# Attention's six middle batches: a hardware loop, or written out one behind the other

## The reference

```python
mod = (silu(c) @ wmod).reshape(8, 6, 1, 256)        # sa, ca, ga, sb, cb, gb
h = layernorm(x) * (1 + ca) + sa
q, k, v = split(h @ W_qkv + b_qkv)                  # 16 heads of 16
scores = q @ k.T / sqrt(16) + rel_bias[clip(i - j + 256, 0, 512)]
x = x + ga * ((softmax(scores) @ v) @ W_out + b_out)
h = layernorm(x) * (1 + cb) + sb
top2 = normalised top 2 of softmax(h @ gate_w.T + expert_bias)
out = layernorm(sum over the two experts of weight * (gelu(h @ w_up) @ w_down)) + h
x = x + gb * out
```

## Time and profile before

| | |
|---|---|
| median of 3 runs | 1375.01 us (1366.27 to 1378.25) |
| the profiled execution | 1366.95 us, its span 1365.3 us |
| mean granted clock of TensorE | 0.911 of full speed |
| busy: PE / PEld / DVE / ACT / POOL | 1129.6 / 896.5 / 803.5 / 640.6 / 864.6 us |
| first score of batch 0; of batch 1; last score of batch 7 | 83.2; 160.9; 779.5 us |

### The profile page before, as it was taken

The page is one execution under the profiler, slowest core; times in us unless marked ns, Lnnn a source line. Parts: engine busy times, 40 slices in busy tenths (PEclk is TensorE's granted clock), DMA queues, the critical chain, the costliest instruction groups (busy, mean ns, idle before and its releaser), DMA issues. The chain is left out here.

```text
span 1365.3 us, 33167 instructions
## 1 busy us (share of the span) xinstructions
PE 1129.6 (83%) x11290; PEld 896.5 (66%) x11291; DVE 803.5 (59%) x2057; ACT 640.6 (47%) x910; POOL 864.6 (63%) x955
## 2 busy tenths in 40 slices
PE   5559999898897998989989851499999999999910
PEld 3236776676676766766767630288888888888810
DVE  4535668467476684675766728555555555555557
ACT  4237776575675765766767611122222222222212
POOL 3235587477575874776756643757666776766656
PEclk9679999899998998999999955599999999999965
DMA  9497674753566447535553217024243344342364
GB/s 310 177 167 228 215 176 123 155 120 97 137 130 118 139 121 154 131 99 137 132 96 137 69 58 277 24 41 108 46 108 82 72 108 101 53 108 46 46 156 130
DMA packets 123113, 168.28 MB, mean 123 GB/s; under 512 B 13016, under 2 KB 99288, under 8 KB 123008
## 3 DMA queue, kind: packets, MB, share of 16 engines
q1 hardware_dynamic: 103136, 137.59, 37.6%
q0 software_dynamic: 19872, 29.15, 11.4%
HBM read 105.74 MB, written 60.96 MB: 122 GB/s over the span
## 5 line engine op out<-in xcount | busy, mean ns | idle before, releaser
L821 DVE CUSTOM_DVE_ANT_0 b_sn<-b_ps_s,s_tile 128x512 f32<-128x512 f32 x512 | 341.5, 688 | 233.7 <-PE b_ps_s L953 230.3
L752 ACT ACTIVATE b_pt<-b_ps_t 128x1024 f32<-128x1024 f32 x256 | 259.1, 1016 | 104.4 <-PE b_ps_t L967 102.6
L967 PE MATMUL b_ps_t<-b_ident,b_sn 128*128 128x128 f32 x2048 | 280.3, 281 | 4.8 <-POOL b_sn L643 3.2
L967 PEld LDWEIGHTS b_ps_t<-b_ident,b_sn 128*128 128x128 f32 x2048 | 248.5, 146 | 45.6 <-issue 16.7
L643 POOL TENSOR_SCALAR b_sn<-b_sn,b_mn 128x512 f32<-128x512 f32 x256 | 175.8, 699 | 145.4 <-DVE b_mn L821 144.7
L1557 ACT ACTIVATE d_g<-d_ps_u 128x512 f32<-128x512 f32 x156 | 92.8, 598 | 319.2 <-PE d_ps_u L1670 309.3
L744 ACT ACTIVATE b_sn<-b_sn,b_mn 128x512 f32<-128x512 f32 x256 | 182.3, 721 | 115.2 <-DVE b_mn L821 108.0
L953 PE MATMUL b_ps_s<-b_ks,b_qs 96*128 96x512 bf16 x512 | 184.8, 397 | 47.6 <-DVE b_mn L821 20.5
L1670 PE MATMUL d_ps_u<-d_xp,k_wu 128*128 128x256 bf16 x1776 | 202.3, 274 | 0.0
L1685 PE MATMUL d_ps_y<-k_wd,d_gp 128*128 128x256 bf16 x1776 | 199.9, 273 | 0.0
L1670 PEld LDWEIGHTS d_ps_u<-d_xp,k_wu 128*128 128x128 bf16 x1776 | 173.9, 99 | 21.8
(11 more groups left out here) (192 smaller groups left out, 1224.2 us busy)
## 6 DMA issues: line engine op xcount, KB each, us to landing
w_parts<-b_w_split SPq DMA_DIRECT2D x32, 512.0 KB, 3.4
splits<-b_parts SPq DMA_DIRECT2D x32, 384.0 KB, 2.6
b_qs<-splits SPq DMA_DIRECT2D x96, 128.0 KB, 6.0
b_ks<-splits SPq DMA_DIRECT2D x96, 128.0 KB, 7.8
b_w_raw<-in_w_up_t SPq DMA_DIRECT2D x16, 512.0 KB, 10.5
b_w_raw<-in_w_down_t SPq DMA_DIRECT2D x16, 512.0 KB, 6.9
k_wu<-w_parts SPq DMA_DIRECT2D x8, 1024.0 KB
k_wd<-w_parts SPq DMA_DIRECT2D x8, 1024.0 KB
```

Source lines behind the costliest of these rows:

```text
L752: act.activation(pt[:, m, 2 * pair:2 * pair + 2, :], ps_t[:, 2 * pair:2 * pair + 2, :], ACT.Exp).then_inc(exped, 1)
L821: dve.tensor_tensor_reduce(sn[:, n % 2, t, :], ps_s[:, t % 2, :], ahead.tile[:, n, at:at + S], -1.0, BIG, ALU.add, ALU.min, mn[:, n % 2, t ...
L967: mm = pe.transpose(ps_t[:, j, t * P:(t + 1) * P], sn[:, m, t, j * P:(j + 1) * P], ident[:, :])
```

## The change

`by_batches` loses its loop: a Python `range` over the eight batches calls `batch` with the same kinds in the same order, so that b is a constant everywhere, and each engine's program holds the middle batch six times. The loop's branch and its register work fall away; the instructions of a batch, their order, their waits' meaning and all tiles stay.

```diff
-        def by_batches(engine, batch):
-
-            batch(0, "first")
-            with engine.Fori(1, B - 1) as b:
-                batch(b, "middle")
-            batch(B - 1, "last")
+        def by_batches(batch):
+
+            for b in range(B):
+                batch(b, "first" if b == 0 else "last" if b == B - 1 else "middle")
...
-            by_batches(sp, batch)
+            by_batches(batch)
...
-            by_batches(pool, batch)
+            by_batches(batch)
...
-            by_batches(act, batch)
+            by_batches(batch)
...
-            by_batches(dve, batch)
+            by_batches(batch)
...
-            by_batches(pe, batch)
+            by_batches(batch)
```

## The result

| | before | changed |
|---|---|---|
| median | 1371.26 us (4 runs, 1366.27 to 1378.25) | 1333.15 us (4 runs, 1329.02 to 1334.35) |
| the profiled execution, its span | 1366.95, 1365.3 us | 1332.73, 1330.9 us |

The ratio is 0.9713 (95% interval 0.9659 to 0.9768): 38.1 us less by the medians, 34.2 us between the two profiled executions. With the further runs of the kernel before that the experiments brought, its median is near 1370 and the gain near 37.

A forecast was written before the change was run, and what follows sets the result against it. TensorE was taken to set each batch's pace, its branch stalls at five seams paid in full. Gain 30.8 us, other terms 0: 1336.2 from the profiled execution, 1344.2 from the median; forecast between them 1341, range 1329 to 1356.

The forecast's parts named there:

- The seam: Last job's start to head 1's first score, between batches: without TensorE's branch 5.65 us each, gaining 30.79 us over five.
- Rival A: At the seams, waits for h1 or the like give back part: 7.4 us, gain 20.2, time 1355; chance 0.14.
- The slow patch: Lower TensorE clock behind head 14's wait: three of six batches kept, cost 0; bounds 4.8 us gained, 3.2 lost.
- Instruction fetch: Written-out engines other than TensorE fetch some 7 packets in each of five more batches; cost taken as 0.
- rival C: Straight code starves DVE, ACT and POOL of instructions: 16.9 us lost a batch, some 1459 us; chance 0.04.
- Register work: Loop register instructions in the engines' sequencers go; no wait for them seen apart from the branch, gain taken as 0.
- Rival B: At the seams only branch time goes, nothing on the path; time stays at 1375; chance 0.04.
- Rival D: The slow patches in the batches vanish too: 4.8 us more gained, 1336 us; chance 0.08 for it or most.
- second stop: TensorE stopping again by "issue" 6.5 us after a seam's first score, for 0.94 us; part of the seam's cost.

The follow-up runs named there:

- e1: Changed kernel, but TensorE alone keeps the hardware loop, the other four engines written out: 1364.81 us, ratio 0.9963 to the kernel before.
- e2: Kernel before, but TensorE alone has its batches written out, the other four keep the loop: 1330.91 us, ratio 0.9708.
- e4: Kernel before, loop on all engines, the product with the values made for one key tile of four: 1318.33 us, one run.
- e9: The kernel before, unchanged, profiled a second time: 1368.09 us.
- e10: The changed kernel, unchanged, profiled a second time: 1330.10 us.
- e7: Changed kernel with the load of h1 moved from head 0 to head 0.5 on GpSimd: 1388.29 us, one run.
- e6: Changed kernel with one of VectorE's four normalising instructions moved from head 13 to 13.5: 1316.0 us, ratio 0.9624 to the kernel before.
- e5: Kernel before, loop on all engines, the product with the values made for three key tiles of four: 1360.31 us, one run.
- e8: TensorE alone in the loop, others written out, and SyncE issues the second stack's twelve loads two heads later: 1406.67 us, one run.

## Why the prediction was right

**The seam.** The step was right in place, cause and end value: 5.65 us was read from the seam without a branch and 5.58 came, six times. e1 and e2 show that TensorE's branch is the cause and the other engines' are not; e4 shows why. The sum over five seams, 30.8 us, came as 30.4 in the stretch that holds them. That close a match is partly luck of the pairing, since both figures take the kernel before from the same profile; between e9 and e10 the same stretch shrank by 37.3 us (463.90 to 426.62).

**The term that was too small.** The gain was 37 to 38 us by medians, where the forecast of 1341 against 1375 makes 34 and the sum 30.8. The price of a branch was taken from one profile that lay low: its five seams sum to 59.04, those of e9 and e1 to 63.96 and 63.8, and with 5.58 us as the end value the excess is 36.1 and 35.9 us, to which the longer heads behind the second gap add 1.2 (e9) and 2.6 (e1). I went halfway between the profiled execution and the median of the runs, 8 us apart, as if either kernel spread like that; part of it is likely a property of the branch, which the change removes. The time came out at 1333.15, 8 us below the forecast and 4 above the range's low end. The narrower reading also fits the narrower spread of the changed kernel (5 us against 12), but e9's other stretches show that the seams are not all of the spread.

**Rival A, h1.** Right to give it a price, and right that it would not come: no seam waited. The slack was read as 3 us; in the changed kernel h1 lands 3.1 to 5.0 us before q0 starts (issue and landing of L554 against the start of L996, batches 2 to 6). e7, which uses the slack up by moving the load 7.1 us, cost 55 us over six batches; the 7.4 us of the prediction could have held only for a load that is late by little.

**The slow patch.** Put at three of six, bounded by none and all. Four of batches 2 to 6 had one in the changed kernel's profile, three in its second. The cost of 0 was right within 1.6 us. Which batches have one remained open: e6 took away the wait and the patches, e7 the patches alone.

**Instruction fetch.** That q8 is TensorE's queue and q14 serves the others is shown by e1 and e2 together: over the whole span q8 has 82 packets and q14 has 40 where the others alone are written out, 68 and 23 where TensorE alone is. No wait of PE came from the new fetches, so rival C fell as reasoned. One sign of it can mislead: in the changed kernel the profile puts seven waits of POOL before b_v, 46.9 us, down to "issue". The kernel before has the same seven, 60.1 us, six of them put down to PE's b_ps_o; e2, whose POOL keeps its loop, has them at the length of the changed kernel (6.6 us a batch), and PE waits for none of them. The count was wrong: 17 packets more on q14, not 35. Of the seven packets of the first pass I took all as the body of one batch; the written-out batches need three to four each.

**Register work.** Put at 0; e2 shows 0.5 us a seam, through DVE at head 0, and seams of 5.58 in place of 5.65 where all is written out. Small and of the right sign.

**Rival B** fell with the result: the whole of the seams' cost came off the time, and no engine needed the idle time that went. Rival D, more patches gone, did not happen here, but came with e6.

**Two readings to correct.** The second stop in the earlier trace rows ends 6.5 us behind the first score; it begins at 5.6. And the prediction has DVE's 56 ns fit the 108 ns that the Trainium skill ("Advanced Engine Details and Errata", Control Flow Timing) gives for a compare-and-branch: 56 is half of it, and TensorE's branch, where its target needed no fetch (e4), took 215, twice as long. The measurements decide, each for its engine.

The landmarks: the last job (L1035, L1033 in the changed kernel) of batches 1 to 6 at 246.2, 332.0, 417.5, 501.9, 587.8 and 673.8 us, forecast from 245.5 to 672.8; the last score at 748.8, forecast 749.

## What to carry to other kernels

In this kernel a hardware loop was dear on the engine with by far the longest body (some 1970 recorded instructions a pass) and nearly free on the others (333 at most). So read the branch's row per engine, and the instruction queues in a window inside the loop. Where a queue went on fetching in every pass, each backward branch stalled its engine while the target came, amid the DMA traffic of the kernel's own loads; the cures seen here are to write the body out, or to make it shorter. And take a recurring price from more than one execution: here the first profile showed 59 us of what was mostly 64.

## What the runs showed of the hardware

- TensorE's backward branch took 215 ns with a body of some 1200 recorded instructions, 4620 with some 1720, and 4460 to 4860 with some 1970 (medians of e4, e5, and of before, e1 and e9). The instruction queue q8 is silent in the first case and fetches 8 packets in 81 us in the second and third. Straight code fetches 7 in that time, without a stop. The Trainium skill ("Runtime: NRT & Kernel Launch", Instruction fetch mechanics) puts TensorE's store at 2048 instructions; by that figure alone the body of e5, and even that of the kernel before, should have been held, and by the measurement neither was.
- By one run, the fetch behind a branch waits in part behind data on the DMA engines: the branch took 3580 ns with them nearly free (e8), 4484 with the twelve loads of 128 KB of the second stack issued around it (e1).
- Of a 6.2 us seam cost, about 3 us are the idle time itself (2.8 to 3.4 at the five seams, 3.26 in the earlier trace rows); the rest follows from it and from the fetch: TensorE works on at half the clock, and a second stop came at three of five seams of the first profile, and at all five of e1 and e9.
- Behind a wait of 2.2 us once a batch the clock fell in 3 of batches 1 to 6 (before), 4 (changed), 3 (e9), 4 (e10) and none (e7, the same wait); with 0.67 us in its place it fell in none (e6). What decides it is open.
